# Extra operations on four engines behind the last work of a routed low-rank kernel

## What is computed

```python
def reference(x, itok, W, b, lora_As, lora_Bs, route_w, A, Bw):
    # x: 8 x 512 x 2048 float32
    y = einsum('bti,oi->bto', x, W) + b                     # 2048 -> 2048
    y = y + 2 * einsum('btr,bro->bto', einsum('bti,bir->btr', x, lora_As[itok]), lora_Bs[itok])   # rank 16, one slot for each batch
    logits = einsum('bsd,ed->bse', y, route_w)              # 8 experts
    route_weight = one_hot(argmax(logits)) * max(logits)    # top 1
    h = einsum('bsd,erd->bser', y, A)                       # 8 experts x rank 16 = 128
    return x + einsum('bser,eor->bso', route_weight[..., None] * h, Bw)
```

## Time and profile before

| what | us |
|---|---|
| median of 2 runs | 305.06 (304.8 and 305.32) |
| the profiled execution: span from the first to the last instruction | 302.6 |
| median less that span | 2.4 |
| TensorE busy | 295.9 (98% of the span) |
| VectorE busy | 193.1 (64%) |
| ScalarE busy | 99.0 (33%) |
| GpSimd busy | 11.0 (4%) |

### The profile page before, as it was taken

The page is one execution under the profiler, slowest core; times in us unless marked ns, Lnnn a source line. Parts: engine busy times, 40 slices in busy tenths (PEclk is TensorE's granted clock), DMA queues, the critical chain, the costliest instruction groups (busy, mean ns, idle before and its releaser), DMA issues.

```text
span 302.6 us, 4629 instructions
## 1 busy us (share of the span) xinstructions
PE 295.9 (98%) x1857; PEld 233.5 (77%) x1857; DVE 193.1 (64%) x258; ACT 99.0 (33%) x147; POOL 11.0 (4%) x37
## 2 busy tenths in 40 slices
PE   7899999999999999999999999999999999999994
PEld 4899999997675885788488758866884787787994
DVE  0160000242894997498579839984985796698775
ACT  0020000223874332534253433424342533322410
POOL 6000300000100000000000000000000000000000
PEclk9999999999999999999999999999999999999999
DMA  7999999999920067739946991998399569536468
GB/s 245 400 404 394 415 412 411 414 417 418 421 107 2 25 252 259 298 133 388 418 172 237 417 405 54 379 395 337 118 377 417 202 220 406 208 151 266 178 218 299
DMA packets 20790, 88.44 MB, mean 292 GB/s; under 512 B 2210, under 2 KB 8354, under 8 KB 12962
## 3 DMA queue, kind: packets, MB, share of 16 engines
q1 hardware_dynamic: 18464, 86.06, 72.4%
q10 hardware_dynamic: 2306, 2.10, 2.0%
HBM read 54.60 MB, written 33.55 MB: 291 GB/s over the span
## 4 chain that ended last, share of the span: by engine, by line
PE 92%; DMA 3%; DVE 3%; SPq 1%; issue 0%
PE bank_out L508 18%; PE bank_h L588 11%; PE bank_h L590 10%; PE bank_h L589 10%; PE bank_e L573 9%; PE bank_out L555 9%; PE bank_out L557 9%; PE bank_out L556 9%; DMA w_ring<-W 3%; DVE x_ring L465 2%; PE bank_l L521 1%; PE bank_r L615 1%; PE bank_l L598 1%; PE bank_h L608 1%; PE bank_h L610 1%; PE bank_h L609 1%
## 5 line engine op out<-in xcount | busy, mean ns | idle before, releaser
L382 DVE TENSOR_TENSOR x_lo<-x_ring,x_hi 128x1024 fp32r<-128x1024 f32 (+1 forms) x72 | 78.9, 1106 | 41.1 <-ACT x_hi L309 41.1
L309 ACT ACTIVATE x_hi<-x_ring 128x1024 fp32r<-128x1024 f32 (+1 forms) x72 | 69.2, 966 | 85.8 <-PE bank_h L590 85.8
L465 DVE TENSOR_TENSOR x_ring<-bank_out,x_ring 128x1024 f32<-128x1024 f32 (+1 forms) x72 | 79.2, 1102 | 1.4 <-PE bank_out L557 1.1
L508 PE MATMUL bank_out<-pt,w_ring 128*128 128x136 f32 x512 | 60.6, 280 | 1.4 <-DMA w_ring<-W 1.4
L508 PEld LDWEIGHTS bank_out<-pt,w_ring 128*128 128x128 f32 x512 | 59.7, 190 | 2.8 <-DMA w_ring<-W 2.5
L588 PE MATMUL bank_h<-x_hi,m_hi 128*128 128x512 f32 (+1 forms) x144 | 55.1, 383 | 0.0
L555 PE MATMUL bank_out<-wh_hi,bw_hi 128*128 128x512 f32 (+1 forms) x144 | 54.6, 379 | 0.0
L590 PE MATMUL bank_h<-x_hi,m_lo 128*128 128x512 f32 (+1 forms) x144 | 53.3, 370 | 0.0
L556 PE MATMUL bank_out<-wh_lo,bw_hi 128*128 128x512 f32 (+1 forms) x144 | 53.2, 369 | 0.0
L557 PE MATMUL bank_out<-wh_hi,bw_lo 128*128 128x512 f32 (+1 forms) x144 | 53.2, 369 | 0.0
L589 PE MATMUL bank_h<-x_lo,m_hi 128*128 128x512 f32 (+1 forms) x144 | 53.1, 369 | 0.0
(11 more groups left out here) (77 smaller groups left out, 130.1 us busy)
## 6 DMA issues: line engine op xcount, KB each, us to landing
x_ring<-xT SPq DMA_DIRECT2D x32, 1024.0 KB, 9.0
outT<-x_ring SPq DMA_DIRECT2D x28, 1024.0 KB, 5.3
w_ring<-W SPq DMA_DIRECT2D x32, 512.0 KB, 9.0
outT<-x_ring SPq DMA_DIRECT2D x16, 256.0 KB, 2.4
pt<-PT SPq DMA_DIRECT2D x4, 272.0 KB, 5.8
x_ring<-loraB ACTq DMA_DIRECT2D x8, 128.0 KB, 10.6
la<-loraA ACTq DMA_DIRECT2D x8, 128.0 KB, 14.3
x_ring<-BwT SPq DMA_DIRECT2D x1, 1024.0 KB, 10.4
```

The lines of the kernel that those rows point to most:

```text
L309: act.activation(out, in_, ACT.Copy).then_inc(done, 1)
L382: dve.tensor_tensor(out, a, b, ALU.subtract).then_inc(done, 1)
L465: dve.tensor_tensor(x, out_banks(u, j), x, ALU.add).then_inc(v_out, 1)
L508: last = mm(bank_out[blk % 2][:, i, 0:PN], w_ring[:, n % WRING, o, i * P:(i + 1) * P], pt[:, k, :], start=(k == 0), stop=(k == C - 1))
```

## The change

Behind the last instruction of their blocks, four engines get more instructions. They read tensors that hold data of the kernel (`la`, `bias_sb`, `bw_hi`, `wh_lo[0]`) or what the new instructions wrote, and write to tensors that are no longer read by the kernel's own work (`m_hi`, `m_lo`, `h_sb`, `wh_hi[0]`, `bank_e`, `bank_h`, `bank_l`). SyncE's program is as before, and nothing ahead of the added instructions is moved. The names `la_2k`, `m_hi_2k` and `m_lo_2k` are halves of 1024 elements for each partition, as `la_1k` and the others are.

```diff
+        f_alone, f_pool, f_act = sem("f_alone"), sem("f_pool"), sem("f_act")
+        v_last, g_last, a_last, t_last = sem("v_last"), sem("g_last"), sem("a_last"), sem("t_last")
+        SIX = 6
         block = ctx.enter_context(nc.Block())
...
                 pool.tensor_copy(ext[u % 2][:, :, E:E + R], la[:, b, :, :]).then_inc(g_ext, 1)
 
+            la_2k = la[:, 4:8, :, :].rearrange("p b c r -> p (b c r)")
+            m_hi_2k = m_hi[:, 8:16, :].rearrange("p c n -> p (c n)")
+            m_lo_2k = m_lo[:, 8:16, :].rearrange("p c n -> p (c n)")
+            pool.wait_ge(f_alone, 1)
+            for k in range(3):
+                pool.wait_ge(g_last, k)
+                pool.tensor_copy(m_hi_2k, la_2k).then_inc(g_last, 1)
+            for k in range(3):
+                pool.wait_ge(g_last, 3 + k)
+                pool.tensor_tensor(m_lo_2k, la_2k, m_hi_2k, ALU.subtract).then_inc(g_last, 1)
+            pool.wait_ge(g_last, 6)
+            pool.tensor_copy(h_sb[:, 16:24], la_2k[:, 0:8]).then_inc(f_pool, 1)
+            for k in range(3):
+                pool.wait_ge(g_last, 6 + k)
+                pool.tensor_tensor(m_lo_2k, la_2k, m_hi_2k, ALU.subtract).then_inc(g_last, 1)
...
                 copy(wh_hi[u % 2][:, 0:nt], h_sb[:, 0:nt], a_wh)
 
+            act.wait_ge(v_last, 12)
+            for k in range(2):
+                act.wait_ge(a_last, 2 * k)
+                act.activation(wh_hi[0][0:GROUP, :], bank_e[0:GROUP, :], ACT.Sign).then_inc(a_last, 1)
+                act.wait_ge(a_last, 2 * k + 1)
+                copy(wh_hi[0][0:GROUP, :], bank_e[0:GROUP, :], a_last)
...
             for j in range(NP2):
                 add_x(NU - 1, j)
+
+            la_1k = la[:, 0:4, :, :].rearrange("p b c r -> p (b c r)")
+            m_hi_1k = m_hi[:, 0:8, :].rearrange("p c n -> p (c n)")
+            m_lo_1k = m_lo[:, 0:8, :].rearrange("p c n -> p (c n)")
+            dve.wait_ge(t_main, NP2 * NU)
+            for k in range(3):
+                dve.wait_ge(v_last, k)
+                dve.tensor_copy(m_hi_1k, la_1k).then_inc(v_last, 1)
+            for k in range(3):
+                dve.wait_ge(v_last, 3 + k)
+                dve.tensor_tensor(m_lo_1k, la_1k, m_hi_1k, ALU.subtract).then_inc(v_last, 1)
+            for k in range(3):
+                dve.wait_ge(v_last, 6 + k)
+                dve.scalar_tensor_tensor(out=m_lo_1k, in0=la_1k, scalar=bias_sb[:, 0:1], in1=m_hi_1k, op0=ALU.mult,
+                                         op1=ALU.add).then_inc(v_last, 1)
+            dve.wait_ge(t_last, 1)
+            for k in range(3):
+                dve.wait_ge(v_last, 9 + k)
+                dve.tensor_scalar(wh_hi[0][0:GROUP, :], bank_e[0:GROUP, :], 0.0, None, ALU.is_gt).then_inc(v_last, 1)
+            dve.wait_ge(v_last, 12)
+            dve.tensor_copy(h_sb[:, 0:8], la_1k[:, 0:8]).then_inc(f_alone, 1)
+            dve.wait_ge(f_pool, 1)
+            for k in range(SIX):
+                dve.wait_ge(v_last, 12 + k)
+                dve.tensor_tensor(m_lo_1k, la_1k, m_hi_1k, ALU.subtract).then_inc(v_last, 1)
...
             for j in range(NP2):
                 out_pair(NU - 1, j)
 
+            pe.wait_ge(a_e, NU)
+            pe.wait_ge(a_h, NU)
+            mm(bank_e[:, :], bw_hi[:, 0:P], wh_lo[0][:, :], start=True, stop=True).then_inc(t_last, 1)
+            last_banks = (bank_h, bank_l)
+            for n in (136, 256, 272):
+                for k in range(8):
+                    mm(last_banks[k % 2][:, 0:n], bw_hi[:, k * P:(k + 1) * P], wh_lo[0][:, 0:n], start=True, stop=True)
+            for k in range(8):
+                n = (272, 136)[k % 2]
+                mm(last_banks[k % 2][:, 0:n], bw_hi[:, k * P:(k + 1) * P], wh_lo[0][:, 0:n], start=True, stop=True)
+            for k in range(8):
+                mm(last_banks[k % 2][:, 0:96], bw_hi[:, k * P:(k + 1) * P], wh_lo[0][:, 0:96], start=True, stop=True)
+            for k in range(8):
+                mm(last_banks[k % 2][:, :], bw_hi[:, k * P:(k + 1) * P], wh_lo[0][:, :], start=True, stop=True)
```

## The result

| | before | changed |
|---|---|---|
| median of the runs, us | 305.06 | 337.83 (337.6 and 338.05) |
| the profiled execution's own time, us | not listed | 337.6 |
| its span, us | 302.6 | 335.6 |

The ratio of the changed kernel's time to that of before is 1.108, with a 95% interval of 1.105 to 1.111: 33 us slower. The forecast was 339.7 us, with a range of 332.5 to 344.5.

A forecast was written before the change was run, and what follows sets the result against it. TensorE was taken to set the pace until the end, where VectorE is last. 299.23 + 12.4 + 10.7 + 14.4 = 336.7, with closing a span of 337.2, 34.6 more; 305.06 + 34.6 = 339.7 us, range 332.5 to 344.5.

The forecast's parts named there:

- end of the last addition: VectorE's tenth closing addition, behind which its new work starts; taken from the earlier trace at 299.23 us.
- VectorE alone: First added stretch: VectorE's casts, subtractions, scalar operations, comparisons and small copy while GpSimd waits; 12.4 us, up to 311.6.
- GpSimd alone: Second added stretch: GpSimd's three casts, three subtractions and small copy while VectorE waits; 10.7 us, up to 322.4.
- both together: Last added stretch: six VectorE and three GpSimd subtractions side by side, their times adding; 14.4 us, up to 336.7.
- behind the last subtraction: Closing barrier at the end of the span, without the row of store waits; some 0.5 us.
- median less span: Median of the runs, 305.06 us, against the span of 302.6; the 2.4 us were carried over unchanged.
- half slope: VectorE's one-input casts of 128x1024 go at two elements a step: 153 + 536 ns, 0.69 us each.
- two composed prices: GpSimd's subtraction of 128x1024: two copies, 2.08 us, or the select's rate plus a second input, 2.45; 2.27 taken.
- Blocking: In the last stretch VectorE and GpSimd each wait for the other's whole instruction: 7.6 + 6.8 = 14.4 us.
- the first rival: VectorE and GpSimd do not block each other in the last part: 7.6 us instead of 14.4, median 332.9; chance 8%.
- cheap GpSimd: Rival: GpSimd's two-input operation goes at a copy's 1.04 us, giving 332.3 us; chance 7%.
- dear conversions: Rival: GpSimd's cast at 2.08 us, VectorE's at 1.22, GpSimd's subtraction at 2.45, giving 345.5 us; chance 8%.

The follow-up runs named there:

- Both kernels once more: Both kernels rerun unchanged: the kernel before took 304.39 us with a span of 302.5, the changed kernel 337.44 us with a span of 335.6.

## Why the prediction was right

The mechanism held step by step but for the overlap at the hand-overs, and the terms were these:

| step | predicted, us | measured, us |
|---|---|---|
| end of the last addition | 299.23 | 298.58 |
| VectorE alone | 12.4 | 12.3 |
| GpSimd alone | 10.7 | 10.8 |
| both together | 14.4 | 13.7 |
| behind the last subtraction | 0.5 | 0.3 |
| span | 337.2 | 335.6 |
| median less span | 2.4 | 2.2 |
| median | 339.7 | 337.8 |

- **VectorE's prices.** Casts 0.690 (taken: 0.69), with a scalar 1.285 (1.29), comparisons out of PSUM 0.679 (0.69, not 0.42). The half slope, read off a difference of 69 ns between two rows of 136 elements, carried over to 1024.
- **GpSimd's prices.** Casts 1.040 (1.04), so fp32r as an output costs nothing more; subtractions 2.338 (2.27, midway between two composed prices). The gaps of GpSimd between dependent instructions were 0.06 to 0.09, not 0.1, and this made up for it by luck. The figure that the prediction quotes from the Trainium skill, GPSIMD Engine Reference, section "Performance versus the Vector engine", 4497 ns for 2048 elements, gives 2.25 as an estimate by halving; the 2.338 measured here are 4% more.
- **Blocking.** Right, and shown by taking it away in three ways (GpSimd quiet, an input from PSUM, fills). The term was 0.7 too large because I charged each instruction whole. The durations alone sum to 3 x 2.34 + 6 x 1.225 = 14.4, but the stretch has five hand-overs from one engine to the other, and at each about 0.14 us overlap.
- **A reading that was wrong.** I wrote of GpSimd's copy that it "got nowhere before VectorE was through". The rows say otherwise: alone it takes 0.40, yet it ended only 0.25 and 0.27 after VectorE's end, so 0.13 to 0.15 of it already lay beside VectorE. And VectorE's next subtraction ended at 79.76, 1.08 after the copy's end at 78.68, where it takes 1.22 alone. With five times 0.14 taken off, the term would have been 13.7.
- **The rest** of the 1.9 us: 0.65 is where the last addition ended, which lies ahead of the change's work and whose cause is open ("Both kernels once more"); 0.2 each are the closing and the time outside the span. I had set one execution's span against the median of others; where a run's own time is listed, 1.8 to 2.8 us lie outside the span, so 2.4 and 2.2 do not tell two kernels apart.
- **The range.** The lower ends that I named (-0.5, -1.1, -0.8) give 337.3, not 336.5. Nothing rests on it, as the range went down to 332.5 for the first rival.
- **What I costed at nothing.** ScalarE's work and the stores are well within their cover. TensorE's work is too, but it needed that cover: without the chain its products cost 2.7 us.
- **The rivals.** Without blocking the last stretch takes 7.5 us; that time exists (with GpSimd quiet, with a PSUM input, with fills), only not in this change. The cheap GpSimd (1.04) and the dear conversions did not occur.

## What to carry to other kernels

When VectorE and GpSimd are to work side by side out of SBUF, add their times rather than take the longer, less some 0.14 us at each hand-over. Two cases tried here need no such sum: VectorE's operation has an input in PSUM, or GpSimd's reads nothing. To find it in a trace, look for one shape of instruction with two durations, and see whether the longer ends a fixed time behind the other engine's instruction. Work hung behind the end of an engine is free only up to its slack: here 3.1 us for VectorE's chain (3.4 less the 0.3 that still stand behind it) and about 4 for TensorE's products.

## What the runs showed of the hardware

- GpSimd, 128 partitions: subtraction of two SBUF tensors 1.26 us for 512 elements and 2.34 for 1024, so 2.1 ns an element on 0.18; cast to fp32r 1.04 for 1024; fill 0.951.
- Who waits for whom: a VectorE subtraction, a three-operand one and a fast cast wait for GpSimd's operations that read SBUF (subtractions, casts, copies) and these for them. VectorE with an input in PSUM and GpSimd did not wait for each other (1.224 and 2.35 us), nor did VectorE's subtractions and a fill (1.225 and 0.951). The Trainium skill, SBUF — State Buffer, section "SBUF: two separate sides", has a shared pair of ports held for the whole instruction. Who blocks whom agreed in all cases tried. The "whole" did not, by the recorded durations: 0.28 to 0.29 us of each pair overlapped whatever the size, by which the last stretch was 13.7 us and not 14.4.
- The two took strict turns as long as both had work queued, in every variant in which they blocked. In these variants each instruction also waits for the one before it on its own engine. Without such waits the rows of the kernel before have one case: GpSimd's copy got in between two subtractions of VectorE.
